# A graph-attention layer: the node part's small fp32 products on half-array TensorE tiles

## What is computed

```python
feats = jnp.maximum(x @ w1 + bb1, 0.0) @ w2 + bb2        # 256 -> 256 -> 64
x_cat = jnp.concatenate([feats[row], feats[col], elem[:, None]], axis=1)   # 129 columns
hid = jnp.maximum(x_cat @ a1 + aab1, 0.0)                # a1 is 129 x 129
e1 = jax.nn.leaky_relu((hid @ a2 + aab2)[:, 0], negative_slope=0.2)
w = jnp.exp(e1 - jnp.max(e1))
pooled = segment_sum(w[:, None] * feats[col], row)
return pooled / (segment_sum(w, row) + 1e-10)[:, None]
```

## Time and profile before

| | before |
|---|---|
| median of 3 runs | 4785.53 us |
| lowest and highest run | 4779.01 and 4790.11 us |
| the profiled execution's own time | 4788.67 us |
| its span | 4786.9 us |
| busy share of the span: PE, DVE, ACT, POOL | 89%, 91%, 80%, 57% |
| mean granted TensorE clock | 0.973 of full speed |

### The profile page before, as it was taken

One profiled execution on the slowest core, in us unless ns is written; L12 is line 12 of the kernel. 1 busy time (PEld: TensorE's weight loads), 2 busy tenths in 40 slices (PEclk: granted clock), 3 DMA queues, 4 the chain that ended last, 5 costly groups with the idle time before them and its releaser, 6 DMA issues.

```text
span 4786.9 us, 131994 instructions
## 1 busy us (share of the span) xinstructions
PE 4257.4 (89%) x24114; PEld 3013.5 (63%) x24115; DVE 4332.7 (91%) x24178; ACT 3831.7 (80%) x12983; POOL 2743.9 (57%) x2886
## 2 busy tenths in 40 slices
PE   1599999999986999999999999999999999999990
PEld 1355555555555777777777777777777777777760
DVE  8789899889896999999999999999999999999988
ACT  1588887888875888888888888888888888888884
POOL 5367777677674555555555555555555555555544
PEclk9999999999998999999999999999999999999995
DMA  2133333333336777777777777777777777777757
GB/s 86 43 81 80 82 86 78 79 88 82 76 81 191 225 225 225 226 224 225 222 225 225 224 224 225 224 225 225 224 225 225 224 225 225 225 224 222 222 163 214
DMA packets 266916, 851.80 MB, mean 178 GB/s; under 512 B 107916, under 2 KB 109584, under 8 KB 266861
## 3 DMA queue, kind: packets, MB, share of 16 engines
q0 software_dynamic: 169920, 673.54, 50.6%
q1 hardware_dynamic: 63543, 160.18, 11.1%
q10 hardware_dynamic: 33398, 17.49, 1.4%
HBM read 739.10 MB, written 111.90 MB: 178 GB/s over the span
## 4 chain that ended last, share of the span: by engine, by line
PE 36%; ACT 26%; issue 3%; DVE 2%; DMA 1%; ACTq 0%; POOL 0%; SPq 0%; DVEq 0%; POOLq 0%
ACT z L1165 18%; PE psum L972 15%; PE psum L976 9%; PE psum L959 8%; ACT onehot L1194 3%; ACT onehot_t L1183 3%; PE psum L985 3%; ACT onehot L1198 2%; DMA p_win<-p_table 1%; PE psum L940 1%; DVE z L1692 1%; DVE z L1685 0%; PE psum L996 0%; ACT onehot L1196 0%; DVE z L1708 0%
## 5 line engine op out<-in xcount | busy, mean ns | idle before, releaser
L755 POOL DMA_INDIRECT z<-qf_table,rec x1664 | 1602.8, 963 | 1468.9 <-PE psum L959 996.7
L1165 ACT ACTIVATE z<-z 128x64 f32<-128x64 f32 x6656 | 1651.5, 336 | 0.0
L972 PE MATMUL psum<-p_win,onehot_t 128*128 x9984 | 1407.8, 275 | 93.1 <-ACT onehot_t L1183 66.5
L972 PEld LDWEIGHTS psum<-p_win,onehot_t 128*128 128x128 bf16 x9984 | 967.0, 97 | 540.0 <-issue 214.2
L959 PE MATMUL psum<-z,onehot 128*128 128x260 f32 x3328 | 1030.3, 391 | 4.7 <-DVE acc L1620 4.0
L976 PE MATMUL psum<-z,ident 128*128 128x258 f32 x3328 | 1002.7, 383 | 0.0
L1571 DVE SCALAR_TENSOR_TENSOR z<-z,a_b 128x129 f32<-128x129 f32 x3328 | 881.6, 289 | 5.9 <-issue 5.0
L1571 DVE SCALAR_TENSOR_TENSOR z<-psum,a_b 128x129 f32<-128x129 f32 x3328 | 828.2, 286 | 0.0
L1561 DVE TENSOR_TENSOR z<-z,psum 128x258 f32<-128x258 f32 x1664 | 699.6, 420 | 105.4 <-PE psum L976 105.0
L1620 DVE TENSOR_TENSOR acc<-acc,psum 125x260 f32 x1664 | 702.0, 422 | 25.3 <-PE psum L959 2.7
L696 POOL DMA_INDIRECT sorted_rows<-z x300 | 491.6, 1639 | 326.7 <-DVE z L1450 231.4
(11 more groups left out here) (220 smaller groups left out, 5584.5 us busy)
## 6 DMA issues: line engine op xcount, KB each, us to landing
p_table<-acc SPq DMA_DIRECT2D x100, 338.6 KB
p_win<-p_table SPq DMA_DIRECT2D x100, 338.6 KB
z<-qf_table,rec POOLq DMA_INDIRECT x1664, 4.5
qf_table<-acc SPq DMA_DIRECT2D x75, 339.5 KB
acc<-in_x_dram SPq DMA_DIRECT2D x25, 448.0 KB
z<-in_x_dram SPq DMA_DIRECT2D x20, 560.0 KB
out_dram<-z ACTq DMA_DIRECT2D x20, 560.0 KB
qf_table<-z SPq DMA_DIRECT2D x25, 339.5 KB
```

Source lines behind the costliest of these rows:

```text
L755: pool.indirect_dma_start(out=z_t[:, o + j, :], out_offset=None, in_=qf_table, in_offset=bass.IndirectOffsetOnAxis(ap=rec[:, o + j, 3:4].b ...
L972: mm = pe.matmul(to, onehot_t[:, j, :], p_flat[:, bass.ds((w % 2) * (3 * ZW) + (part * ZW + o), n)], start=(part == 0), stop=(part == 2 an ...
L1165: op = act.activation(z_t[:, slot, o:o + DO], z_t[:, slot, o:o + DO], ACT.Copy, scale=z_t[:, slot, o + DO:o + HF])
```

## The change

The second layer and the p and q products no longer use zero-padded operands. `feats` takes the weights of one head (64 columns) and writes 64 output partitions; the two heads of a pair follow each other as two tiles of the array, one on its left and one on its right 64 columns. `p_product` and `q_product` take the 64 feature rows of one head as stationary operand and 129 or 193 moving columns; the two heads of a pair follow each other as tiles on the upper and the lower 64 rows of the array, and write into two different banks (5 and 6, or 2 and 3), chosen by the head's place in its pair and no longer by the pair. The numbers of matmul instructions in `feats` stay at 8 per group; those of `p_product` and `q_product` go from 2 to 4 per window, with half the columns. ACT and DVE read the same number of values from the banks with other strides, into the same places. The two clearing instructions of POOL, SP's wait for them and the zero padding go; the copy of the identity is two instructions of 64 partitions.

```diff
-        w2_s = carve(MC * P).rearrange("p (m n) -> p m n", m=MC)
-        ad_at = used[0]
-        ad_p = carve(2 * HALF).rearrange("p (q n) -> p q n", q=2)
-        ad_q = carve(2 * (HALF + P)).rearrange("p (q n) -> p q n", q=2)
+        w2_s = carve(MC * DO).rearrange("p (m n) -> p m n", m=MC)
+        ad_p = carve(2 * AT).rearrange("p (q n) -> p q n", q=2)
+        ad_q = carve(2 * (AT + DO)).rearrange("p (q n) -> p q n", q=2)
...
-            sp.wait_ge(s_const, 2)
             for m in range(MC):
                 h, c = m // (HID // P), m % (HID // P)
-                sp.dma_start(w2_s[:, m, (h % 2) * DO:(h % 2 + 1) * DO], W2[h, c * P:(c + 1) * P, :]).then_inc(s_weights, 16)
+                sp.dma_start(w2_s[:, m, :], W2[h, c * P:(c + 1) * P, :]).then_inc(s_weights, 16)
...
-            pool.memset(w2_s, 0.0).then_inc(s_const, 1)
-            pool.memset(acc[:, ad_at:ad_at + 2 * (2 * HALF + P)], 0.0).then_inc(s_const, 1)
...
             pool.wait_ge(s_weights, N_W)
-            pool.tensor_copy(ad_q[:, 0, HALF:HALF + P], ident[:, :]).then_inc(s_const, 1)
-            pool.tensor_copy(ad_q[:, 1, HALF:HALF + P], ident[:, :]).then_inc(s_const, 1)
+            pool.wait_ge(s_row_field, 1)
+            for r in range(2):
+                own = slice(r * DO, (r + 1) * DO)
+                pool.wait_ge(s_const, 15 + r)
+                pool.tensor_copy(ad_q[own, :, AT:AT + DO], ident[own, own].unsqueeze(1).to_broadcast([DO, 2, DO])).then_inc(s_const, 1)
...
-            def feats(g, m):
-                q = m // (MC // 2)
-                if m == 0:
+            def feats(g, q, c):
+                if q == 0 and c == 0:
                     since(pe, s_p_ev, g * 4)
-                pe.wait_ge(s_h_ev, g * MC + m + 1)
-                mm = pe.matmul(psum[:, 5 + q, 0:NG], w2_s[:, m, :], h_t[:, m, :], start=(m % (MC // 2) == 0), stop=(m % (MC // 2) == MC // 2 - 1))
-                if m % (MC // 2) == MC // 2 - 1:
+                pe.wait_ge(s_h_ev, g * MC + (q * 4 + c + 3))
+                for r in range(2):
+                    mm = pe.matmul(psum[r * DO:(r + 1) * DO, 5 + q, 0:NG], w2_s[:, q * 4 + r * 2 + c, :], h_t[:, q * 4 + r * 2 + c, :],
+                                   start=(c == 0), stop=(c == 1), skip_group_check=True)
+                if c == 1:
                     mm.then_inc(s_f_mm, 1)
...
                 for q in range(2):
-                    mm = pe.matmul(psum[0:WN, 5 + q, 0:HALF], f_t[:, q, at], ad_p[:, q, :], start=True, stop=True)
+                    for r in range(2):
+                        own = slice(r * DO, (r + 1) * DO)
+                        mm = pe.matmul(psum[0:WN, 5 + r, q * AT:(q + 1) * AT], f_t[own, q, at], ad_p[own, q, :], start=True, stop=True)
                 mm.then_inc(s_p_mm, 1)
...
                 for q in range(2):
-                    mm = pe.matmul(psum[0:WN, 2 + q, 0:HALF + P], f_t[:, q, at], ad_q[:, q, :], start=True, stop=True)
+                    for r in range(2):
+                        own = slice(r * DO, (r + 1) * DO)
+                        mm = pe.matmul(psum[0:WN, 2 + r, q * (AT + DO):(q + 1) * (AT + DO)], f_t[own, q, at], ad_q[own, q, :], start=True, stop=True)
                 mm.then_inc(s_q_mm, 1)
...
-            beside = {1: [(-1, p_product, 3), (0, hidden, 0)], 2: [(0, hidden, 1)], 3: [(0, hidden, 2), (0, feats, 0)],
-                      4: [(0, hidden, 3), (0, feats, 1)], 5: [(0, hidden, 4), (0, feats, 2)], 6: [(0, hidden, 5), (0, feats, 3)],
-                      7: [(0, hidden, 6), (0, feats, 4)], 8: [(0, hidden, 7), (0, feats, 5)], 9: [(0, feats, 6), (0, feats, 7)],
+            beside = {1: [(-1, p_product, 3), (0, hidden, 0)], 2: [(0, hidden, 1)], 3: [(0, hidden, 2)],
+                      4: [(0, hidden, 3), (0, feats, 0, 0)], 5: [(0, hidden, 4), (0, feats, 0, 1)], 6: [(0, hidden, 5)],
+                      7: [(0, hidden, 6)], 8: [(0, hidden, 7), (0, feats, 1, 0)], 9: [(0, feats, 1, 1)],
...
-                act.activation(qf_out[w][0:WN, 0:ZW].rearrange("p (q n) -> p q n", q=2), psum[0:WN, 2:4, 0:HALF], ACT.Copy)
...
+                act.activation(qf_out[w][0:WN, 0:ZW].rearrange("p (q r n) -> p r q n", q=2, r=2), of[:, :, :, 0:AT], ACT.Copy)
```

More of the change, by code:

```diff
@@ L491, in _ @@
                 sp.dma_start(w1_s[:, k, :, :], W1[:, k * P:(k + 1) * P, :].rearrange("h p n -> p h n")).then_inc(s_weights, 16)
-            sp.wait_ge(s_const, 2)
             for m in range(MC):
                 h, c = m // (HID // P), m % (HID // P)
-                sp.dma_start(w2_s[:, m, (h % 2) * DO:(h % 2 + 1) * DO], W2[h, c * P:(c + 1) * P, :]).then_inc(s_weights, 16)
+                sp.dma_start(w2_s[:, m, :], W2[h, c * P:(c + 1) * P, :]).then_inc(s_weights, 16)
             for h in range(H):
                 for u in range(2):
-                    sp.dma_start([ad_p, ad_q][u][(h % 2) * DO:(h % 2 + 1) * DO, h // 2, (h % 2) * AT:(h % 2 + 1) * AT],
+                    sp.dma_start([ad_p, ad_q][u][(h % 2) * DO:(h % 2 + 1) * DO, h // 2, 0:AT],
                                  A1[h, u * DO:(u + 1) * DO, :]).then_inc(s_weights, 16)
@@ L635, in _ @@
             pool.iota(chunk_id, [[P, 3]], base=0, channel_multiplier=1, allow_small_or_imprecise_dtypes=True).then_inc(s_const, 1)
-            pool.wait_ge(s_const, 13)
+            pool.wait_ge(s_const, 11)
             pool.affine_select(out=ident[:, :], in_=ident[:, :], pattern=[[-1, P]], compare_op=ALU.not_equal,
@@ L641, in _ @@
                                fill=0.0, base=-1, channel_multiplier=-1).then_inc(s_const, 1)
-            pool.wait_ge(s_const, 15)
+            pool.wait_ge(s_const, 13)
             pool.tensor_copy(ident_b, ident[:, :]).then_inc(s_const, 1)
@@ L787, in _ @@
         def _(pe):
-            pe.wait_ge(s_const, 20)
+            pe.wait_ge(s_const, 18)
             def count_windows(g):
@@ L917, in group @@
                             place(g, b, part)
-                    for off, product, n in beside.get(q, []):
+                    for off, product, *n in beside.get(q, []):
                         if not isinstance(g, int) or 0 <= g + off < GROUPS:
-                            product(g + off, n)
+                            product(g + off, *n)
             sort_loop(pe, group)
@@ L1043, in _ @@
             act.wait_ge(s_weights, N_W)
-            act.wait_ge(s_const, 19)
+            act.wait_ge(s_const, 17)
             act.wait_ge(s_tables, 1)
@@ L1103, in take_q @@
                 since(act, s_qf_st[w], g * 32)
-                act.activation(qf_out[w][0:WN, 0:ZW].rearrange("p (q n) -> p q n", q=2), psum[0:WN, 2:4, 0:HALF], ACT.Copy)
-                act.activation(qf_out[w][0:WN, ZW:QW].rearrange("p (q r f) -> p q r f", q=2, r=2)[:, :, :, 0:DO],
-                               psum[0:WN, 2:4, HALF:HALF + P].rearrange("p q (r f) -> p q r f", r=2), ACT.Copy).then_inc(s_q_ev, 1)
+                of = psum[0:WN, 2:4, 0:2 * (AT + DO)].rearrange("p r (q n) -> p r q n", q=2)
+                act.activation(qf_out[w][0:WN, 0:ZW].rearrange("p (q r n) -> p r q n", q=2, r=2), of[:, :, :, 0:AT], ACT.Copy)
+                act.activation(qf_out[w][0:WN, ZW:QW].rearrange("p (q r f) -> p r q f", q=2, r=2)[:, :, :, 0:DO],
+                               of[:, :, :, AT:AT + DO], ACT.Copy).then_inc(s_q_ev, 1)
             beside = {0: [(take_x,)], 1: [(take_h, 0)], 2: [(take_h, 1)], 3: [(take_h, 2)], 4: [(take_h, 3)], 5: [(take_h, 4)], 6: [(take_h, 5)],
@@ L1274, in _ @@
             dve.tensor_copy(edge_lo[0:EP, :], ui).then_inc(s_edge_step, 1)
-            dve.wait_ge(s_const, 17)
+            dve.wait_ge(s_const, 15)
             dve.wait_ge(s_masks, 2)
@@ L1456, in p_sum @@
                 since(dve, s_p_lo, n - 1)
-                dve.tensor_tensor(p_f[0:WN, w % 2, :].rearrange("p (q n) -> p q n", q=2), psum[0:WN, 5:7, 0:HALF],
-                                  ab1_b[0:WN, :].rearrange("p (q n) -> p q n", q=2), ALU.add).then_inc(s_p_ev, 1)
+                dve.tensor_tensor(p_f[0:WN, w % 2, :].rearrange("p (q r n) -> p r q n", q=2, r=2),
+                                  psum[0:WN, 5:7, 0:HALF].rearrange("p r (q n) -> p r q n", q=2),
+                                  ab1_b[0:WN, :].rearrange("p (q r n) -> p r q n", q=2, r=2), ALU.add).then_inc(s_p_ev, 1)
             beside = {11: [(0, p_sum, 0)], 13: [(0, p_sum, 1)], 15: [(0, p_sum, 2)], 1: [(-1, p_sum, 3)]}
```

## The result

| | before | after |
|---|---|---|
| median | 4787.41 us (4 runs) | 4699.68 us (4 runs, 4696.90 to 4703.86) |
| ratio, 95% interval | | 0.982 (0.9808 to 0.9832) |
| span of the profiled execution | 4786.9 us | 4700.1 us |
| mean granted TensorE clock | 0.973 | 0.962 |

What follows compares the result with a forecast made beforehand. PE was taken to set the time from step 1 to step 11 and DVE the rest; the terms gave -0.37 us per group on PE's leg, -9 us over 25 groups, so 4777 us, with a range from 4735 to 4825.

Steps and rivals of the forecast that it cites:

- What bounds the kernel: Node and sorting part: PE sets the time from step 1 to step 11, then DVE; gain limited to 3.9 us per group.
- The switch: Full array to tiles and back: 0.09 us in and 0.09 out, plus the weight load that lies bare.
- Do two tiles run at once?: Second layer, p and q: only the next head's first record may start beside the previous head's second, once its weights are loaded.
- 4827: No-overlap form in the second layer alone, loads bare: +0.40 per pair, +42 us in all; chance 0.05 of the 0.25.
- Second layer: Steps 4, 5, 8, 9: a pair takes 1.57 us with switches in place of 1.68, -0.44 us per group.
- Step 10's q: q product in step 10: way in covered by a wait for ACT, way out 0.11, net -0.08 us per group.
- Step 11: q then p in one tiled stretch: -0.19 - 0.02 + 0.11 = -0.10 us per group.
- Step 1: p before the first layer: way out +0.17 us, taken as +0.25 per group because the clock is often at half.
- The better overlap: Rival: tiles overlap better than strict order allows, loads side by side; -1.6 us per group, -40 us, 4745; chance 0.20.
- its fullest form: Better overlap with second-layer pairs wholly in two record times: another 1.7 us per group, hardly below 4711; outside the range.
- the rival without overlap: Steps 4 to 9 mainly: tiles do not overlap, drains stay; +1.5 us per group, +38 us, 4824; chance 0.25.
- The clock: Rival around a group's start: half clock lasts 3.4 us longer in half of the groups, +21 us, 4798; chance 0.10.

Runs made afterwards that it cites:

- the half first layer in the kernel before: The kernel before with the first layer over 128 of its 256 features only: 4694.46 us.
- the lone tile: The kernel before with each second-layer product on a 64-column tile in its old place, without a partner on the other tile: 4841.49 us, ratio 1.0114.
- the merged pairs: The changed kernel with the two second-layer pairs of each bank in one stretch (steps 5 and 9): 4691.36 us, ratio 0.9800.
- the kernel head by head: The changed kernel with p and q ordered as both upper-row products first, then both lower-row ones, in place of alternating: 4705.33 us, ratio 0.9832.

## Why the prediction was wrong

- **What bounds the kernel: right in the main.** Two legs, PE's from step 1 to step 11, and a gain limited by DVE's waits, 3.9 us per group. The change took 3.65; the half first layer in the kernel before took 92 us of 94, though not all of it out of these waits.
- **The switch: right.** 0.09 in, and 0.24 for the way in, out and the bare load, by the lone tile and the merged pairs.
- **"Do two tiles run at once?": the step that failed.** I took strict order between the heads: the second head's first record beside the first head's second, its load behind. The evidence was that loads and matmuls stand in strict order in every row; but all those rows are of one tile at a time, so they bear on the order within a tile, and not on two. The pair cut at 800.23 shows that loads and records of two tiles start together, and the kernel head by head that a tile at the start of a stretch does not wait for the other tile's list. The prediction's own sign of better overlap, q in 0.8 us, came: 0.76. The Trainium skill had this overlap (TensorE: Matmul & The Clock Gate, Part 3: matmuls on different tiles start about 4 ns apart); the trace agrees, within the 0.01 us that its rows resolve. The Trainium skill's rule of the same part, that loads overlap running matmuls only where their rows differ, is the one that the prediction put beside its 4827; the trace disagrees again, since all four loads of the pair have started by 800.30, while both tiles' first records, begun at 800.23 on the same 128 rows, are under way.
- **So the terms of the sum were mis-sized.** Second layer: -0.11 per pair forecast, 1.08 in place of 1.68 measured (from 800.14, where the first layer is through, to 801.22), -0.60, so -2.4 for four. Step 10's q: -0.08 forecast, 0.85 in place of some 1.40, -0.55. Step 11: -0.10 forecast, 1.30 in place of 2.27, -0.97, of which 0.53 came back as PE's longer wait for ACT. "The weight loads eat the gain" of p was wrong: the loads of the two tiles run side by side.
- **Step 1** was forecast at +0.25; measured it is +0.05, from two shifts against each other. PE's timeline of one group (p, the first layer, the prefix), before from 870.88 and after from 868.84:

```profile
870.88 1.82 PE L878 MATMUL psum<-acc 128*125 128x258 f32 x4 [0.32 <-DVE acc L1457]
872.53 1.84 PE L858 MATMUL psum<-acc 128*128 128x500 f32 x4
874.22 0.33 PE L824 MATMUL psum<-z,before 127*128 127x400 bf16 x1
...
868.84 0.80 PE L879 MATMUL psum<-acc 64*125 64x129 f32 x8 [0.62 <-DVE acc L1461]
869.57 3.50 PE L856 MATMUL psum<-acc 128*128 128x500 f32 x4
872.91 0.34 PE L822 MATMUL psum<-z,before 127*128 127x400 bf16 x1
```

  Over the 24 groups, p up to the first layer takes 1.06 us on average where it took 1.62, -0.56, and the first layer behind it 3.08 where it took 2.47, +0.61. In the groups shown, p is the slow one before and the first layer after: its four records take 3.34 in place of 1.69 us, with a granted clock of 0.64 from 868.80 to 873.50, partly at the lower of its two levels. With this the terms give -3.3 of the -3.65 us; the rest is not assigned.
- **Evacuations with new strides** were put at nothing, rightly: the copies take as long as before.
- **The rivals.** The better overlap was there, with its mechanism and even the cap, but with a chance of 0.20; and its fullest form was left out of the range as a mere bound. That bound is given as 4711, while its own terms, -1.6 and -1.7 us over 25 groups, make 4703, nearer to the 4699.68 that came. (The terms of the rival without overlap add up to 1.6 us per group and not 1.5, which moves its 4824 by 2 to 3 us.) What I missed is that nothing stood against it but rows of another kind. The lone tiles show what switches without overlap cost: 55 us more, in another arrangement than that of the slower rival, which was put at 38.
- **The clock.** It fell for longer, as that rival said (mean 0.973 to 0.962). Its cost shows in step 1's first layer, +0.61 us per group, but p became faster there by nearly as much, so the step came out even.

## What to carry to other kernels

Half-array tiles paid here only with a partner beside them in the list: a pair cost 0.99 us where one lone tile cost 0.98 and one full-array product 0.84, and each stretch of tiles pays about 0.24 us for its way in and out, so tiled products belong together. When a trace holds one kind of work only, rows of that kind don't decide between the two ends of an unknown price; keep both ends in the range. And before an engine is relieved, read how long the others wait for it: 94 us of waits for PE went with gains of 88 and 92 us, by two quite different cuts.

## What the runs showed of the hardware that was not expected

- Two fp32 products on the left and right 64 columns of the array, with different moving data through the same 128 rows, run side by side at full speed: both first records at 800.23, 0.99 us for the pair against 0.98 for a lone tile.
- The fp32 weight loads of two tiles run side by side too; two row tiles with 125-column loads and 129 moving columns each need 0.54 us for eight records with the way out, less than their eight loads of 0.10, which make 0.80, would need one after the other.
- At the start of a stretch a tile's first record does not wait for the other tile's two products that stand ahead of it in the list (both first records at 808.08, head by head); behind other tiled work its first load did wait, until 811.84 in place of 811.68. Whether two row tiles may write one bank was not tried; the change gives them two.
